# Elementwise bounds moved from VectorE to GpSimd, with new call lists, in a fused attention and feed-forward block on one core

## The chip, the cores and the metric

The kernel runs on one core of a Trainium2 chip. The metric is the device time in microseconds (us) of one execution. The engines are TensorE (PE; its weight loads are a row of their own, PEld), VectorE (DVE), ScalarE (ACT), GpSimd (POOL) and SyncE (SP), which here only issues DMAs. Each engine works through its own list of instructions in order; semaphores order the engines against each other.

## What is computed

The input `x` has 4 batches of 256 tokens with 256 channels. Two stages each add to it:

```python
def _bi_wkv(r, k, v, w, u, time_emb):            # k = v = fside, time_emb = cond
    tf = sigmoid(sum(time_emb, -1))[:, None, None]
    decay = exp(-exp(w))[None, :] * (0.5 + 0.5 * tf[:, :, 0])
    ek = exp(minimum(k, 30.0));  ekv = ek * v
    # forward and backward recurrences a = a*decay + ekv, b = b*decay + ek over the tokens
    euk = exp(minimum(u + k, 30.0))
    num = nf + nb - ekv + euk * v
    den = df + db - ek + euk
    return sigmoid(r) * (num / maximum(den, 1e-8)) * (0.8 + 0.2 * tf)

x = x + attn(_bi_wkv(x, fside, fside, w1, u1, cond), ...)   # Mamba-2 style: in_proj, causal conv, SiLU,
                                                           # 8 heads, decayed causal scores, RMS norm, gate, out_proj
x = x + ffn(_bi_wkv(x, fside, fside, w2, u2, cond), ...)    # ternary weights, 8-bit activations,
                                                           # 256 -> 1024, SiLU, GELU, layer norm, 1024 -> 256
# weight_quant: round(w / mean|w|) clipped to -1..1
```

The kernel applies `minimum(k, 30)` after the exponential, as a minimum with exp(30).

## The kernel before

The work is split by batch `b` = 0 to 3, and from the residual on by row block `i` = 0 to 7 of 128 tokens (two for each batch). Every engine has a set of small functions, one for each step, and under them a list of calls, which is the order of its work. The list of each engine mixes steps of different batches, so that the feed-forward of batch 0 runs beside the attention of batches 1 to 3. Nothing else orders the work: an engine whose next call waits for a semaphore does nothing until it comes. `HOME` gives each TensorE result its PSUM bank.

The steps that this document speaks of, in the order of the data:

- ACT `wkv_exp(b)` (L691) writes `E`, the exponential of `k`, one instruction of 128x512. ACT `wkv_own(b)` (L698) writes `own`, exp(u+k) for both stages, four instructions.
- DVE `wkv_min(b)` (L1192, its instruction L1195) and `own_min(b)` (L1197, L1199) bound the two with exp(30), one instruction each. POOL `times_v(b)` (L476, L480) and `own_times_v(b)` (L483, L487) multiply them with `v`. Only one pair of buffers exists for each, so a pair serves batches b and b+2.
- DVE `forward(b, w, k)` and `backward(b, w, k)` are the recurrences, each a scan of 128x514 (L1209, L1218), four of each for a batch: w is the stage, k the denominator (0) or the numerator (1). `forward(b, w, 0)` waits for the bound, `forward(b, w, 1)` for the product with `v`. They also wait for `D`, the decay factors, made for batches 1 to 3 by ACT `make_D` and `make_turn`, the latter from POOL `turn_decay` and DVE `make_decay` and `make_gap`. `add_own` (L1229) joins them with `own` into `nd`.
- ACT `recip_seed` (L734 to L738), DVE `recip` (L1237, L1240), `ratio` (L1246) and POOL `second_ratio` (L493) divide. ACT `gate_x` (L744) makes tanh(x/2), and DVE `gated(b)` (L1256) writes `uT`, the input of the attention part, on which TensorE's `features(b)`, `conv_in` and `gate_in` wait.
- From PE `features(b)` ACT and DVE make scores' factors and, through `softplus_log` and `softplus_out`, the log decays `la`. PE `running_sums(b)` sums them, ACT and DVE `running_sums(b)` split the sums, SP `spread_sums(b)` copies them into `cum_t` with six DMAs (L347), and PE `log_decays(b, c, g)` waits for them. PE `scores(b)` waits for the masks `late` and `tri` of POOL. ACT `decays` takes exponentials (L836), DVE `attend` (L1326) multiplies, PE `within` and `between` make the output, with POOL `state_values` (L500) before `between`.
- DVE `conv_taps` (L1302) is the convolution, six instructions for half a batch.
- `residual(p)`, `gate_h`, `ffn_in`, `norm_h` (POOL, L504 to L526), `ffn_in_scale`, `quantise_h` (POOL, L534) and PE `q1_turns(p)` prepare the feed-forward input of part p (batches 0 to 2 whole, batch 3 in two halves: p = 3 and 4). PE `ffn_up(i)` needs POOL `ffn_diag(i)` (L474); ACT `ffn_silu`, `ffn_gelu`, `ffn_var`, DVE `ffn_center`, `ffn_shift`, `ffn_max`, ACT `ffn_square`, POOL `ffn_dev`, `ffn_rms`, `ffn_round` (L568), SP `turn_q2(i)` (a DMA transpose), PE `ffn_down(i)`, DVE `ffn_out(i)` and SP `store(i)` are the rest.
- Both weights lie in `wn`. ACT `weight_abs(i)` (L683) sums their absolute values, PE `weight_sums`, DVE `weight_mean`, POOL `weight_round(i)` (L466), DVE `clip_weights(i)` (L1188, L1190) and ACT `weight_done(i)` (L689) quantise them, each instruction 128x2048.

PE `warm(k)` are eight matmuls on constants whose result nobody reads. ACT's functions come from several table sets; a `preload_act_table_set` call loads one (24 of them before).

The lists stand at L347 and after for SP, L571 for POOL, L927 for ACT, L1449 for DVE, L1834 for PE. Two pieces of the lists before, around the places that the prediction comes to:

```python
# ACT, first part                     # POOL, middle
recip_seed(0, 0, 1)                   state_values(2)
weight_abs(0)                         ffn_dev(0)
recip_seed(0, 1, 2)                   norm_h(1)
make_D(1)                             quantise_h(1)
```

## Time and profile before

| | |
|---|---|
| median of 3 runs | 205.1 us (204.43 to 205.75) |
| the profiled execution: its time | 205.91 us |
| its span, first to last instruction | 203.8 us |
| mean granted TensorE clock | 0.908 |
| instructions | 3179 |

The profile is of one execution, which took 0.8 us more than the median of the runs; 2.1 us of its time lie outside the span. Times in the rows are microseconds from the start of the span, unless marked ns.

### The profile page before, as it was taken

The page shows a single profiled execution, that of the slowest core. Times are in us where ns is not written, and L with a number is a line of the kernel's source. Part 1 is how long each engine was busy: PE and PEld are TensorE (multiplying, and loading weights), DVE is VectorE, ACT ScalarE, POOL GpSimd, SP SyncE. Part 2 cuts the span into 40 slices and gives each one's busy share as a digit, 9 for nine tenths or more (in the row PEclk, how much of TensorE's full clock was granted, in tenths as well). Part 3 has the DMA queues.
Part 4 walks back from the last instruction along what each step waited for, and adds up shares of the span by engine and source line. Part 5 has one row for each costly group of instructions (what it writes and reads, how often), then busy time and mean ns, then how long its engine had stood idle before and what let it go on. Part 6 is the DMA issues. An engine that isn't in the chain of part 4 may idle for free.

```text
span 203.8 us, 3179 instructions
## 1 busy us (share of the span) xinstructions
PE 163.1 (80%) x904; PEld 120.7 (59%) x908; DVE 178.1 (87%) x315; ACT 162.2 (80%) x295; POOL 100.5 (49%) x172
## 2 busy tenths in 40 slices
...
DVE  1899999999999999999999999998667777986952
...
GB/s 114 365 387 396 238 2 2 3 0 2 206 0 3 0 0 2 5 2 0 2 4 1 0 0 0 5 0 0 47 12 0 51 0 10 68 31 116 64 77 51
DMA packets 12304, 11.55 MB, mean 57 GB/s; under 512 B 7680, under 2 KB 10368, under 8 KB 12032
## 3 DMA queue, kind: packets, MB, share of 16 engines
...
q8 instruction: 7, 0.11, 0.2%
q10 hardware_dynamic: 432, 0.03, 0.2%
...
## 4 chain that ended last, share of the span: by engine, by line
PE 60%; DVE 19%; issue 8%; ACT 7%; POOL 4%; POOLq 1%; DVEq 0%; ACTq 0%
PE banks L1659 55%; PE banks L1656 5%; DVE Fs L1209 4%; DVE Ys L1218 4%; DVE nd L1229 2%; DVE banks L1409 1%; DVE decay L1153 1%; DVE wn L1417 1%; DVE tn L1237 1%; POOL wn L568 1%; ACT banks L890 1%; ACT banks L886 1%; ACT wn L912 1%; POOL gap_r L438 1%; DVE dtp L1282 1%
## 5 line engine op out<-in xcount | busy, mean ns | idle before, releaser
L1659 PE MATMUL banks<-inw,uT 128*128 128x8 f32 (+1 forms) x64 | 20.4, 444 | 16.7 <-DVE uT L1256 16.7
L1659 PEld LDWEIGHTS banks<-inw,uT 128*128 128x128 f32 x64 | 11.2, 215 | 23.0 <-issue 22.6
L1209 DVE TENSOR_TENSOR_SCAN Fs<-D,E 128x514 f32<-128x514 f32 x16 | 21.0, 1334 | 0.6 <-POOL D L441 0.5
L1659 PE MATMUL banks<-uT,inw 128*128 128x256 f32 x80 | 20.2, 397 | 0.0
L1302 DVE SCALAR_TENSOR_TENSOR cv<-banks,cols,cv 128x255 f32<-128x255 f32 (+2 forms) x48 | 19.3, 470 | 0.0
L1218 DVE TENSOR_TENSOR_SCAN Ys<-D,Fs 128x514 f32<-128x514 f32 x16 | 18.9, 1203 | 0.0
L500 POOL TENSOR_TENSOR vs<-vv,grow 128x512 f32<-128x512 f32 x4 | 4.5, 1131 | 28.5 <-issue 18.3
L1659 PEld LDWEIGHTS banks<-uT,inw 128*128 128x128 f32 x80 | 15.2, 197 | 3.1 <-issue 1.4
L1659 PEld LDWEIGHTS banks<-vv,skips 128*128 128x128 f32 x128 | 15.2, 192 | 2.1 <-issue 2.0
L1659 PE MATMUL banks<-w2T,wn 128*128 128x256 f16 x64 | 10.4, 320 | 7.6 <-DMA wn<-wn 7.6
L1659 PE MATMUL banks<-b1b,diag 128*128 128x512 f32 x32 | 15.1, 595 | 0.6 <-POOL diag L474 0.6
L1659 PE MATMUL banks<-vv,skips 128*128 128x64 f32 x128 | 15.4, 274 | 0.3 <-ACT vv L794 0.3
L1659 PE MATMUL banks<-vv,dec 128*128 128x64 f32 x128 | 15.6, 275 | 0.0
L1659 PEld LDWEIGHTS banks<-vv,dec 128*128 128x128 f32 x128 | 14.9, 192 | 0.0
L1659 PE MATMUL banks<-outw,yzT 128*128 128x256 f32 x64 | 14.7, 380 | 0.0
L1659 PE MATMUL banks<-starts 128*128 128x256 bf16 x80 | 12.7, 324 | 2.0 <-POOL starts L421 2.0
L1659 PEld LDWEIGHTS banks<-w2T,wn 128*128 128x128 f16 x64 | 7.3, 116 | 10.6 <-DMA wn<-wn 7.9
L1409 DVE SCALAR_TENSOR_TENSOR banks<-banks,nmu,xcT 128x1024 f32<-128x1024 f32 x8 | 10.3, 1288 | 3.2 <-issue 2.5
L1659 PEld LDWEIGHTS banks<-outw,yzT 128*128 128x128 f32 x64 | 11.8, 190 | 1.9 <-issue 0.5
L480 POOL TENSOR_TENSOR E<-E,vT 128x512 f32<-128x512 f32 x4 | 5.8, 1456 | 13.1 <-DVE E L1195 13.1
L487 POOL TENSOR_TENSOR own<-own,vT 128x1024 f32<-128x1024 f32 x4 | 11.2, 2790 | 1.7 <-DVE own L1199 1.7
L1659 PEld LDWEIGHTS banks<-starts 128*128 128x128 bf16 x80 | 9.1, 116 | 4.3 <-POOL starts L421 2.0
...
## 6 DMA issues: line engine op xcount, KB each, us to landing
...
```

Of the source, the lines that this page charges most:

```text
L438: pool.tensor_tensor(gap_r[:, :, :, 0], gap[:, :, :, 0], mhalf[:, 0:2 * CT].rearrange("p (w c) -> p w c", w=2), ALU.pow).then_inc(turn_ok, 1)
L480: pool.tensor_tensor(E[:, b % 2, 1, :, 0:T], E[:, b % 2, 0, :, 0:T], vT[:, b].rearrange("p (c t) -> p c t", c=CT), ALU.mult).then_inc(ev_o ...
L487: pool.tensor_tensor(own[:, b % 2, :, 1, :], own_e(b), vT[:, b].unsqueeze(1).broadcast_to([P, 2, CT * T]), ALU.mult)\
L500: pool.tensor_tensor(by_head(vs[:]), by_head(vv[:, b % 2, 0]), grow[:, 0, :].unsqueeze(2).broadcast_to([P, NH, HD]), ALU.mult).then_inc(vs ...
L568: pool.tensor_scalar(Q2[:, i % 2], Y[:, i % 2], qq[:, i:i + 1], ROUND16, ALU.mult, ALU.add)\
L1209: dve.tensor_tensor_scan(Fs[:, w, k], D[:, w, 0:CT * TS], E[:, b % 2, k].rearrange("p c t -> p (c t)"), 0.0, ALU.mult, ALU.add).then_inc(f ...
L1218: dve.tensor_tensor_scan(Ys[:, w, k][:, ::-1], D[:, w, 1:CT * TS + 1][:, ::-1], Fs[:, w, k][:, ::-1], 0.0, ALU.mult, ALU.add).then_inc(ys_ ...
L1229: last = dve.scalar_tensor_tensor(nd[:, :, w, s], y, gap[:, w, ct, b:b + 1], own[:, b % 2, w, :, s], ALU.mult, ALU.add)
L1302: dve.scalar_tensor_tensor(cv[:, ft, back:], at("conv_in", b, i)[:, j * T:(j + 1) * T - back], cols[:, w:w + 1], cv[:, ft, back:], ALU.mul ...
L1409: dve.scalar_tensor_tensor(ffn_mid(i), ffn_mid(i), nmu[:, i:i + 1], lngb, ALU.add, ALU.mult)\
L1656: return pe.transpose(dst, src, ident[0:n, 0:n])
L1659: return pe.matmul(dst, lhsT, rhs, start=start, stop=stop)
```

## The change

1. `wkv_min(b)` for b = 1 to 3 and `own_min(b)` for b = 1 to 3 run on POOL, as a tensor_scalar with two operations (minimum with exp(30), maximum with 0). `wkv_min(0)` and `own_min(0)` stay on DVE. The POOL functions wait in addition for the bound of the batch before.
2. `clip_weights(0)` and `clip_weights(1)` run on POOL.
3. The call lists of SP, POOL, ACT, DVE and PE are new throughout, and with them the PSUM banks in `HOME` and the bare waits between PE's calls. Nothing else of the functions changes. There are 25 table loads on ACT: two more in the first part, one less around `ffn_gelu(2)`.

The diff, cut to what the text speaks of:

```diff
 # SP: order of the loads
 load_cond()
 load_k(0)
-load_xT(0)
-load_x(1)
+load_b1()
+load_x(2)
 load_xT(2)
 load_k(1)
-load_x(2)
 load_k(2)
+load_w1()
+load_x(0)
+load_x(1)
 load_xT(1)
...
+load_xT(3)
+load_xT(0)
+load_w2()
+load_inw()
+spread_sums(0)
+load_k(3)
+load_b2()
...
 turn_q2(0)
 turn_q2(1)
+store(0)
 turn_q2(2)
 turn_q2(3)
+turn_q2(4)
 store(1)
-store(0)
+turn_q2(5)
 store(2)
-turn_q2(4)
-turn_q2(5)

 # POOL
+def clip_weights(i):
+    pool.wait_ge(wrnd_ok[i], 1)
+    pool.tensor_scalar(wn[:, i], wn[:, i], ROUND + 1.0, ROUND - 1.0, ALU.min, ALU.max).then_inc(wclip_ok[i], 1)
+
+def wkv_min(b):
+    pool.wait_ge(e_ok, b + 1)
+    pool.wait_ge(emin_ok, b)
+    e = E[:, b % 2, 0, :, 0:T]
+    pool.tensor_scalar(e, e, EXP_MAX, 0.0, ALU.min, ALU.max).then_inc(emin_ok, 1)
+
+def own_min(b):
+    pool.wait_ge(own_ok, b + 1)
+    pool.wait_ge(omin_ok, b)
+    pool.tensor_scalar(own_e(b), own_e(b), EXP_MAX, 0.0, ALU.min, ALU.max).then_inc(omin_ok, 1)
...
-make_ident()
 make_starts()
 make_masks()
+make_late()
+make_ident()
 first_turn()
 times_v(0)
 own_times_v(0)
-make_rows()
 turn_decay()
+wkv_min(1)
 times_v(1)
+own_min(1)
 make_tri()
+own_times_v(1)
 second_ratio(0)
-own_times_v(1)
+make_rows()
+wkv_min(2)
 times_v(2)
-make_late()
 second_ratio(1)
+own_min(2)
+wkv_min(3)
 state_values(0)
...
 norm_y(0, 0)
+weight_round(0)
 norm_y(0, 1)
-weight_round(0)
 state_values(1)
+own_min(3)
+residual_bias(0)
+clip_weights(0)
 times_v(3)
...
 state_values(2)
+weight_round(1)
 ffn_dev(0)
+clip_weights(1)
 norm_h(1)
+norm_y(2, 0)
 quantise_h(1)
...
 quantise_h(3)
-ffn_round(2)
 ffn_round(3)
+ffn_dev(4)
 ffn_diag(6)
-ffn_dev(4)
 norm_h(4)
 quantise_h(4)

 # ACT, first part
 wkv_exp(0)
+spread_heads()
+wkv_exp(1)
 wkv_own(0)
 wkv_own(1)
...
+weight_abs(0)
+act.preload_act_table_set("natural_log_exp_and_others")
+recip_seed(0, 0, 1)
+make_D(1)
+make_turn(1)
+recip_seed(0, 1, 2)
+act.preload_act_table_set("exp_and_others")
 gate_x(0)
+make_skips()
+weight_abs(1)
+features(0)
+wkv_own(2)
 exp_a()
 act.preload_act_table_set("natural_log_exp_and_others")
...
 # ACT, around ffn_gelu(2)
 act.preload_act_table_set("silu_and_others")
+silu_z(3, 0)
 ffn_silu(2)
 running_sums(3)
+weight_columns()
+silu_conv(3, 0)
+turned_y(2, 1)
 act.preload_act_table_set("gelu_and_others")
 ffn_gelu(2)
-act.preload_act_table_set("silu_and_others")
-silu_z(3, 0)

 # DVE: clip_weights gone, wkv_min and own_min called for batch 0 alone; first part
+wkv_min(0)
+out_factor()
 first_D()
-wkv_min(0)
 forward(0, 0, 0)
-own_min(0)
-backward(0, 0, 0)
-make_decay()
 forward(0, 0, 1)
 forward(0, 1, 0)
+backward(0, 0, 0)
+own_min(0)
 backward(0, 0, 1)
+make_decay()
 forward(0, 1, 1)
+make_gap()
 add_own(0, 0)
 backward(0, 1, 0)
 backward(0, 1, 1)
-make_gap()
 add_own(0, 1)
-out_factor()
 recip(0, 0, 1)
-own_min(1)
 ratio(0)
-wkv_min(1)
+forward(1, 0, 0)
 gated(0)
 recip(0, 1, 2)
-forward(1, 0, 0)
 forward(1, 0, 1)
...
-softplus_in(0)
 features(0)
+forward(1, 1, 0)
+backward(1, 0, 0)
+softplus_in(0)
+forward(1, 1, 1)
+backward(1, 0, 1)
 softplus_out(0)
...
 running_sums(0)
-wkv_min(2)
 conv_taps(0, 1)
 recip(1, 0, 2)
 conv_taps(0, 0)
 ratio(1)
-own_min(2)
 gated(1)

 # PE, last part (before: ffn_down(0) ahead of project(4), ffn_down(1) and (2) ahead of ffn_up(7))
 ffn_up(5)
+project(4)
 ffn_down(0)
-project(4)
 q1_turns(3)
+ffn_down(1)
 ffn_up(6)
-ffn_down(1)
-ffn_down(2)
 q1_turns(4)
 ffn_up(7)
+ffn_down(2)
```

## Rows read from the trace of the kernel before

**Rows 1.** The page: busy time of the engines; DVE's busy tenths and DMA rate in 40 slices.

```profile
PE 163.1 (80%) x904; PEld 120.7 (59%) x908; DVE 178.1 (87%) x315; ACT 162.2 (80%) x295; POOL 100.5 (49%) x172
...
DVE  1899999999999999999999999998667777986952
...
GB/s 114 365 387 396 238 2 2 3 0 2 206 0 3 0 0 2 5 2 0 2 4 1 0 0 0 5 0 0 47 12 0 51 0 10 68 31 116 64 77 51
```

**Rows 2.** Stretches: from:to, length, busy time of each engine (x instructions), clock, DMA share, GB/s.

```profile
80.00:100.00 20.00, 20.00 (x129) 16.47 (x128) 19.67 (x37) 17.07 (x37) 15.72 (x16) 1.00 0.01 2
...
137.00:150.00 13.00, 12.97 (x56) 7.82 (x55) 9.57 (x17) 11.80 (x19) 6.15 (x10) 1.00 0.11 21
```

**Rows 3.** The chain that ended last, in order of time: start, us, what.

```profile
45.86 0.41 DVE cum_s L1321
46.27 0.35 DVE E L1195
48.18 0.30 POOL late L432
48.53 3.03 PE banks L1659 x11
51.69 1.44 PE banks L1659 x3
```

**Rows 4.** Groups of DVE instructions by shape: busy, mean ns of one.

```profile
L1218 DVE TENSOR_TENSOR_SCAN Ys<-D,Fs 128x514 f32<-128x514 f32 x16 | 18.9, 1203 | 0.0
L1199 DVE TENSOR_SCALAR own<-own 128x1024 f32<-128x1024 f32 x4 | 2.7, 677 | 0.0
L1190 DVE TENSOR_SCALAR wn<-wn 128x2048 f32<-128x2048 f32 x2 | 2.4, 1211 | 0.0
L1195 DVE TENSOR_SCALAR E<-E 128x512 f32<-128x512 f32 x4 | 1.7, 419 | 0.0
```

**Rows 5.** Groups of POOL instructions by shape, the nearest to the moved ones.

```profile
L534 POOL TENSOR_SCALAR h<-h,hq 128x256 f32<-128x256 f32 x8 | 4.7, 588 | 3.3 <-DVE hq L1387 3.3
L466 POOL TENSOR_SCALAR wn<-wn,wrec 128x2048 f32<-128x2048 f32 x2 | 3.9, 1974 | 0.7 <-DVE wrec L1186 0.5
```

**Rows 6.** Timeline of POOL and DVE side by side around 10 us: start, us.

```profile
10.46 3.19 POOL L487 TENSOR_TENSOR own<-own,vT 128x1024 f32<-128x1024 f32 x1 [1.75 <-DVE own L1199]
11.44 2.63 DVE L1153 TENSOR_SCALAR decay<-fdec,eew 128x3 f32<-128x3 f32 x4
```

**Rows 7.** Timeline of the first part, around `gated(0)`

```profile
11.91 0.61 ACT L744 ACTIVATE th<-xcT 128x512 f32<-128x512 f32 x1
...
12.64 1.28 ACT L940 ACT_TABLE_LOAD   x1
...
25.29 0.63 ACT L738 ACTIVATE Ys<-Ys 128x512 f32<-128x512 f32 x1
...
26.86 0.68 DVE L1256 SCALAR_TENSOR_TENSOR uT<-th,nd 128x512 f32<-128x512 f32 x1
...
33.03 0.84 DVE L1265 SCALAR_TENSOR_TENSOR bcf<-banks,bcr 64x256 f32<-64x256 f32 x2
...
33.76 2.43 ACT L815 ACTIVATE skips<-ident,heads 128x128 f32<-128x128 f32 x8
...
36.10 1.90 ACT L683 ACTIVATE dec<-wn 128x2048 f32<-128x2048 f32 x1
```

**Rows 8.** POOL's timeline around 117 us.

```profile
117.11 1.04 POOL L500 TENSOR_TENSOR vs<-vv,grow 128x512 f32<-128x512 f32 x1 [14.82 <-issue]
...
121.45 0.19 POOL L504 TENSOR_SCALAR hmv<-hss 128x2 f32<-128x2 f32 x1 [0.81 <-ACT yzT L874]
```

**Rows 9.** Timeline around 171 us, DVE and POOL.

```profile
166.66 0.42 DVE L1362 SCALAR_TENSOR_TENSOR h<-h,R 128x256 f32<-128x256 f32 x1 [1.22 <-ACT h L862]
...
170.64 2.32 POOL L568 TENSOR_SCALAR wn<-wn,qq 128x1024 f16<-128x1024 f32 x2
...
171.95 1.28 DVE L1362 SCALAR_TENSOR_TENSOR h<-h,R 128x256 f32<-128x256 f32 x1
```

More of the change, by code:

```diff
@@ L30 @@
 HOME = {
-    "warm": (6, 2, 1, 5, 0, 4, 4, 3, 3, 6),
+    "warm": (7, 3, 2, 0, 6, 2, 4, 2, 5, 0),
     "cond_sum": 1,
-    "weight_sums": 7,
-    "features": (7, 2, 1, 3),
-    "conv_in": ((5, 2), (5, 6), (4, 2), (0, 4)),
-    "conv_turns": ((2, 5), (7, 5), (5, 2), (3, 2)),
-    "gate_in": ((0, 6), (6, 4), (7, 4), (2, 5)),
-    "r2_turns": (4, 0, 5, 4),
-    "scores": (1, 3, 3, 4),
-    "log_decays": (((7, 4), (3, 7)), ((1, 6), (7, 4)), ((5, 1), (0, 2)), ((2, 3), (6, 7))),
-    "running_sums": (3, 1, 1, 1),
-    "within": ((4, 2), (5, 6), (5, 2), (6, 5)),
-    "between": (3, 5, 4, 3),
-    "y_turns": ((3, 1), (2, 0), (7, 2), (2, 4)),
-    "project": (2, 2, 4, 3, 5),
-    "q1_turns": (3, 6, 7, 3, 6),
-    "ffn_up": (6, 0, 6, 0, 6, 0, 4, 6),
+    "weight_sums": 2,
+    "features": (0, 3, 6, 3),
+    "conv_in": ((5, 3), (6, 6), (2, 7), (4, 2)),
+    "conv_turns": ((6, 5), (1, 6), (4, 3), (3, 4)),
+    "gate_in": ((4, 0), (0, 3), (3, 2), (2, 5)),
+    "r2_turns": (7, 5, 5, 3),
+    "scores": (1, 5, 5, 2),
+    "log_decays": (((4, 6), (3, 4)), ((2, 4), (1, 0)), ((1, 0), (4, 3)), ((4, 3), (3, 6))),
+    "running_sums": (6, 1, 1, 4),
+    "within": ((7, 7), (2, 4), (4, 5), (7, 4)),
+    "between": (3, 7, 3, 2),
+    "y_turns": ((4, 4), (0, 4), (6, 0), (5, 5)),
+    "project": (7, 3, 1, 2, 4),
+    "q1_turns": (7, 7, 6, 2, 4),
+    "ffn_up": (6, 0, 6, 0, 6, 0, 2, 6),
     "weight_columns": 5,
-    "ffn_turns": ((0, 0), (0, 0), (0, 0), (0, 0), (0, 0), (0, 0), (3, 4), (5, 6)),
-    "ffn_down": (2, 2, 3, 0, 1, 2, 7, 0),
+    "ffn_turns": ((0, 0), (0, 0), (0, 0), (0, 0), (0, 0), (0, 0), (2, 3), (6, 7)),
+    "ffn_down": (3, 5, 4, 0, 1, 5, 4, 0),
 }
```

475 lines of the change are left out of this document (222 added, 253 removed).

## The prediction

> **What bounds the kernel now.** I read the page first, then stretches, then the chain, then timelines.
>
> The page [rows 1] shows no single bound: DVE is busy 87% of the span, PE and ACT 80%, POOL 49%. DVE's slices say when: nines from about 8 us to 138 us, sixes and sevens after that. The change takes work off DVE, so the question is whether DVE sets the end while it is full. The stretches [rows 2] answer it: from 80 to 100 us PE is busy 20.00 of 20 us at full clock, and DVE 19.67. Both are full. The chain [rows 3] runs through DVE up to 46 us (the split of the running sums, then a bound of `E`), through POOL's mask `late`, and from 48.53 us on PE, which it does not leave for long before 168 us. The list of PE's work is the same in sum before and after. So from 50 to 168 us a freed DVE gives nothing unless PE gets its work in another order or sooner, and the places to cost are the first 50 us, the steps that PE waits for, and the tail.
>
> **Part 1: the bounds and the clip leave DVE.** DVE loses three bounds of `own` (3 x 0.677), three of `E` (3 x 0.419) and two clips (2 x 1.211): 2.03 + 1.26 + 2.42 = 5.7 us [rows 4]. POOL gains the same eight instructions. No row shows a minimum on POOL. The nearest has the size and form of the clip: 1.974 us for 128x2048 [rows 5], by columns 0.99 us for 1024 and 0.49 us for 512, in sum 2 x 1.97 + 3 x 0.99 + 3 x 0.49 = 8.4 us. The other end is the 128x256 row, 0.588 us [rows 5], which by columns gives 4.70, 2.35 and 1.18, in sum 20 us. I take 8.4, since its row is of the clip's own size. POOL has 103 us free, so the sum fits; where it stands in the queue matters (below). On DVE, 1.1 of the 5.7 us stand before `gated(0)` (bounds of batch 1) and 4.6 later. What it is worth: at least 0, since PE covers it; at most 4.6 less the holds that the new POOL work puts on DVE.
>
> Such holds are in the trace: while POOL multiplied `own` from 10.46 to 13.65 us, four DVE instructions of three elements took 2.63 us together and ended 0.4 us after it [rows 6]; four more places look so. The Trainium skill, page "SBUF — State Buffer", section "Who interferes with whom", says that a DVE instruction with two SBUF inputs and a GpSimd instruction that reads SBUF exclude each other for the whole instruction. By that rule each moved bound that falls among scans holds DVE longer (0.99 us) than it did on DVE (0.677); by the rows of the three-element instructions alone one would expect a hold only now and then. It is a rival below.
>
> **Part 2: the first part, by the new lists.** Up to `add_own(0, 1)` DVE has the same work, in another order. The second seed on ACT, three steps of 0.63, follows it and ended at 25.92 [rows 7], so `add_own(0, 1)` ended at 24.0, and does now. From there to `uT` at 26.86 [rows 7] stood `recip(0, 0, 1)`, `ratio(0)` and two bounds (1.1), so the first two are 1.8 us. With `forward(1, 0, 0)` (1.2, as the other scans of [rows 4]) they end at 27.0. `gated(0)` also waits for tanh, and ACT's second seed has no reason to end sooner than 25.9. Behind it come a table load (1.28) and `gate_x(0)` (0.61) [rows 7], which before was done at 12.5: 25.9 + 1.3 + 0.6 = 27.8. `uT` of batch 0 starts at 27.8 to 28.2 instead of 26.86, 1.0 to 1.3 us late. ACT then makes the skips (2.43, [rows 7]) and the second weight sum (about 2.1) before `features(0)`, which starts near 32.7 and lets DVE's `features(0)` start at about 33.6 instead of 33.03 [rows 7]. DVE idles some 2 us before it. From there to the end of `add_own(1, 1)` stand four forward and backward pairs less the two forwards done (six scans, 7.2 us), and the short softplus and `add_own(1)`, which I estimate from the sizes in [rows 4] at 0.8 and 2.7: 33.6 + 0.8 + 7.2 + 0.8 + 2.7 = 45.1. Before, it ended at about 45.1 too, since the split of the sums behind it (1.2 us) ended at 46.27 [rows 3]. The relief of 1.1 us is spent on the wait for tanh. The loads: `in_w` comes last but one now, yet all loads together were through by 25 us (five slices of 5.1 us, [rows 1]), before PE needs it at 28.
>
> PE waited for `late` until 48.53 [rows 3], since POOL stood in its queue behind a bound of DVE. Now `late` is made at once. But the next step, `log_decays(0)`, waits for the sums that DVE ended at 46.27 and for six DMAs, and started at 51.69 [rows 3]. DVE ends those sums at 46.2 again, so the DMAs and `log_decays(0)` come at 51.6. Scores done early only lengthen the wait. Part 2 is worth 0; bounds: 1.1 us sooner (if tanh is not late) and 2 us later (if DVE's idle time adds to the wait).
>
> **Part 3: the middle.** The new lists load one table less around `ffn_gelu(2)`: 1.28 us of ACT (row of [rows 7]), in a stretch where ACT is busy 11.80 of 13 us but PE 12.97 of 13 [rows 2]. Between 0 and 1.28 I take the middle, 0.6 us gained. The two loads more in the first part are in part 2.
>
> **Part 4: the tail.** `ffn_in(4)` on DVE took 1.28 us beside POOL's two roundings, 170.64 to 172.96 [rows 9]; the other instruction of its size took 0.42 [rows 9]. Now one of the two is done sooner, so of the 0.86 us held I take 0.6 as gained, between 0 and 0.86. `project(4)` ahead of `ffn_down(0)` ends 1 us sooner on PE, but ACT reaches `gate_h(4)` only after `ffn_gelu(4)`, which waits for `ffn_up(5)` whose place is the same: 0. `store(1)` now stands behind the transposes of blocks 2 to 4 and the waits of their roundings; `ffn_out(3)`, which needs its buffer, is called after them: 0.
>
> **Sum.** 0 + 0 - 0.6 - 0.6 = -1.2 us. On the profiled execution 205.91 - 1.2 = 204.7, a span of 202.6; that execution was 0.8 above the median, so the median comes to 205.1 - 1.2 = 203.9 us. A change below 1% (2.05 us) is about what a measurement of this kernel can't tell from none, and this is below it. With the bounds of the parts the likeliest case itself reaches from 202 (1.1 + 1.28 + 0.86 = 3.2 gained) to 207.1 (2 lost).
>
> **Rivals.**
> - Rival A, the relief shows. If PE's fullness is one that follows DVE (PE gets each batch as DVE delivers it), 4.6 us come off, less two bounds of `own` that hold scans for 0.99 each: 2.6 net, and the 1.2 above: 201.3 us. For it: DVE is full from 8 to 138 us, the chain before 46 us is DVE's, and the lists are new on all engines, so PE may get the next batch sooner. Against: PE shows no idle time at all in [rows 2]. In its best form (all 4.6 and 1.2) 199.3.
> - Rival B, POOL's queue becomes late: the slower side. At 117.11 us POOL starts `state_values(2)`, having waited; `norm_h(1)` follows at 121.45 with 0.81 us to spare [rows 8]. Now `weight_round(1)` and `clip_weights(1)`, 1.97 each, stand between them, so `norm_h(1)` starts 3.9 - 0.8 = 3.1 us later, then `quantise_h(1)`, `q1_turns(1)` and the blocks 2 and 3 of the feed-forward, which PE's list has in a fixed place; `weight_done(1)` on ACT also waits. If PE stands still for it: 205.1 + 3.1 - 0.6 = 207.6 us (part 4's gain is kept). It decides when `state_values(2)` starts later than about 114 us. For it: POOL idled 14.8 us before 117.11 and now puts the work behind that wait instead of into it. Against: PE has `conv_in(3)` and `features(3)` to do meanwhile.
> - Rival C, the exclusion: of the 8.4 us of new POOL work, the part of batches 1 and 2 (2 x 0.99 + 2 x 0.49 = 3.0 us) falls where DVE does little but scans, and holds it in full, against 2 x (0.677 + 0.419) = 2.2 saved. DVE's first 60 us then get 0.8 us longer, and with the late tanh not covered (1.3) and -1.2: 205.1 + 0.8 + 1.3 - 1.2 = 206.0 us. For it [rows 6]; against, other POOL work beside scans left them at 1.2 us. This is what the rule of the skill named above would do here, and the trace agrees with it in part.
>
> **Chances.** Forecast 0.40, A 0.31, B 0.17, C 0.12. Faster by over 1% (below 203.05): 0.04 from the forecast's lower end, 0.28 from A, in sum 0.32. Slower by over 1% (above 207.15): 0.02, 0.15 from B, 0.05 from C, in sum 0.22. The rest, 0.46, is within 1%. The range that leaves 2 in 10 out reaches to A's centre and a little under it, and to B's: 200.5 to 207.7 us.
>
> **What the changed profile would show.** Part 1: DVE busy near 172 us; POOL near 109, with the clip at 1.9 to 2.1 us; the bounds at 1.0 and 0.5. If the clip is over 4 us, the cost of POOL is wrong and B grows. Part 2: `uT` first written at about 28 us with DVE idle before it, released by ACT's tanh; `add_own(1, 1)` ending near 45 us; the first `log_decays` near 51.6. Sooner than 50 refutes part 2 and speaks for A. Part 3: one table load less from 137 to 150 us, PE full from 57 to 167 us. PE idle for over 2 us before `ffn_up(2)` or `q1_turns(1)` would be B. Part 4: `ffn_in(4)` at 0.42 us. If PE stays without idle time and yet its last `ffn_up` ends over 3 us sooner than before, my reading of PE as the bound was wrong.

## The result, and the profile after

The changed kernel takes 209.8 us (median; runs 207.91, 209.81 and 209.89) against 205.1 us: a ratio of 1.0185 with an interval of 1.0129 to 1.0242. Measured again later, six runs lay between 208.0 and 210.2 us, beside eleven of the kernel before from 204.4 to 206.9: 1.0174 (1.0122 to 1.0226). The profiled execution took 209.89 us, its span is 207.8. It is nearly 2% slower; 203.9 was forecast, and 209.8 lies outside the range. Below, a time is the median of all runs of a kernel, and the brackets behind it give the ratio to the kernel before with its 95% interval. The ratio leaves out runs over 1.5% above the fastest of their kernel, so the two can stand apart, most of all in `g_tail` and `g_warm`, where 7 of 12 and 9 of 13 runs are left out.

The page of the kernel after, busy time of the engines as in [rows 1]:

```profile
span 207.8 us, 3188 instructions
PE 162.0 (78%) x903; PEld 119.1 (57%) x908; DVE 175.2 (84%) x307; ACT 164.1 (79%) x296; POOL 118.1 (57%) x180
```

DVE lost its eight instructions and POOL has eight more, 17.6 us of busy time instead of the 8.4 forecast; the span is 4.0 us longer. Groups of instructions by shape, after (busy, mean ns of one), beside [rows 4, 5]:

```profile
L478 POOL TENSOR_SCALAR wn<-wn 128x2048 f32<-128x2048 f32 x2 | 4.6, 2296 | 0.2
L489 POOL TENSOR_SCALAR own<-own 128x1024 f32<-128x1024 f32 x3 | 3.8, 1251 | 0.3
L484 POOL TENSOR_SCALAR E<-E 128x512 f32<-128x512 f32 x3 | 2.6, 854 | 18.3 <-ACT E L718 18.2
```

The moved work itself is 4.6 + 3.8 + 2.6 = 11.0 us, including the time in which it was held itself (a hold is time by which an instruction beside one of the other engine takes longer than it does alone). Most of the other 6.6 us comes from one instruction on 128x1 that otherwise takes 0.19 us and here took 8.44; some other rows of POOL are shorter than before. Timeline of POOL and DVE, after:

```profile
104.26 8.44 POOL L519 TENSOR_SCALAR ymv<-yss 128x1 f32<-128x1 f32 x1
104.34 1.20 DVE L1231 TENSOR_TENSOR_SCAN Fs<-D,E 128x514 f32<-128x514 f32 x1
...
109.95 2.70 DVE L1251 SCALAR_TENSOR_TENSOR nd<-Ys,gap,own 128x512 f32<-128x512 f32 x4
```

It began 0.08 us before a run of back-to-back scans and ended 0.05 us after the last product behind them.

Where does the time of the end come from? I read the same milestones in both timelines (ends, in us):

```
                         before  after  later by
uT of batch 0              27.5   31.3   3.7
add_own(1, 1)              45.1   47.6   2.5
split of the sums, b 0     46.3   49.3   3.0
within(1)                  95.9   99.2   3.3
within(2)                 126.2  129.8   3.6
within(3)                 159.6  163.5   3.8
project(3)                164.8  168.2   3.4
ffn_up(7)                 181.0  184.4   3.4
span                      203.8  207.8   4.0
```

The loss is there at 50 us and is only carried from then on: PE is busy 19.96 of 20 us from 80 to 100 us, as full as in [rows 2], and can catch up nothing. The last half microsecond is in the last two products, both `ffn_down`: they took 1.84 us each, at a granted clock of 1.2 GHz, and 1.72 and 1.04 us in the kernel before.

The trace of the later repetition (210.17 us, span 208.4) has DVE's work within 0.1 us of the first up to 60 us, and `log_decays` starts at 54.70 in both. But its clock comes back to 2.4 GHz at about 64.2 us and not at 58.1, so that `ffn_up(7)` ends at 186.6, 2.2 us later still, and then its last two products run at 2.4 GHz, 1.04 us each, which gives 1.6 us back. So 3.0 us of the loss are in the order of the work and stand in both traces; what comes on top of them changes with the clock from run to run.

The stretch that loses it, around `gated(0)`, POOL and DVE side by side, after; it answers to [rows 7]:

```profile
22.72 0.99 POOL L484 TENSOR_SCALAR E<-E 128x512 f32<-128x512 f32 x1
23.16 1.09 DVE L1259 SCALAR_TENSOR_TENSOR tn<-nd,Ys 128x512 f32<-128x512 f32 x1
23.79 1.58 POOL L495 TENSOR_TENSOR E<-E,vT 128x512 f32<-128x512 f32 x1
24.28 1.64 DVE L1262 SCALAR_TENSOR_TENSOR Ys<-tn,Ys 128x512 f32<-128x512 f32 x1
25.46 1.36 POOL L489 TENSOR_SCALAR own<-own 128x1024 f32<-128x1024 f32 x1
25.95 1.40 DVE L1268 SCALAR_TENSOR_TENSOR nd<-nd,fout,Ys 128x512 f32<-128x512 f32 x1
27.28 1.31 DVE L1231 TENSOR_TENSOR_SCAN Fs<-D,E 128x514 f32<-128x514 f32 x1
27.48 3.25 POOL L502 TENSOR_TENSOR own<-own,vT 128x1024 f32<-128x1024 f32 x1
28.51 2.76 DVE L1278 SCALAR_TENSOR_TENSOR uT<-th,nd 128x512 f32<-128x512 f32 x1
```

Read it as a handing over of turns. Each DVE instruction with two inputs ends 0.53 to 0.55 us after the POOL instruction beside it: `tn` at 24.25 after 23.71, `Ys` at 25.92 after 25.37, the ratio at 27.35 after 26.82, and `uT` at 31.27 after 30.73. Alone they take 0.69, 0.69, 0.74 and 0.68 us, as the same four do in the kernel before, where nothing of POOL of that kind stands beside them. These four and the scan took 8.2 instead of 4.0 us.

From `tn` on, the kernel before has such holds as well, 3.0 us of them, but all behind `uT`: `tn` of 1.75 us, two scans of 3.19 instead of 2.3 us, and a product of 128x16, `dtp`, of 1.31 instead of 0.15 us. Timeline of DVE, before:

```profile
27.46 1.75 DVE L1237 SCALAR_TENSOR_TENSOR tn<-nd,Ys 128x512 f32<-128x512 f32 x1
...
29.85 3.19 DVE L1209 TENSOR_TENSOR_SCAN Fs<-D,E 128x514 f32<-128x514 f32 x2
```

That difference in place is the one that counts. PE waits for `uT` to make the features of batch 0, and DVE needs those features about 5 us later. The chain that ended last, after (start, us, what), in the place of [rows 3]:

```profile
28.51 2.77 DVE uT L1278
...
31.42 3.77 PE banks L1671 x12
...
44.49 3.06 DVE nd L1251 x4
...
52.89 1.68 DMA cum_t<-cum_s
...
54.70 2.30 PE banks L1671 x5
```

And the two ends of it in the timeline, DVE idle for the features, PE for the decays:

```profile
36.08 0.85 DVE L1287 SCALAR_TENSOR_TENSOR bcf<-banks,bcr 64x256 f32<-64x256 f32 x2 [2.33 <-ACT bcr L782]
...
47.92 0.91 DVE L1341 CAST cum_s<-crest 40x256 bf16<-40x256 f32 x1
...
54.70 0.58 PE L1671 MATMUL banks<-cum_t,cum_s 99*128 99x512 bf16 x1 [7.73 <-DMA cum_t<-cum_s]
```

The sum, from the start of `tn` to the end of the split: DVE began `tn` at 23.16, 0.76 us sooner than before. Holds were 4.6 us (the 4.2 above and 0.35 in `add_own`) instead of 3.0 (+1.6), two bounds are gone (-1.1), DVE idled 2.33 us for the features (+2.3), and the cast of the sums took 0.91 instead of 0.28 us beside POOL's bound and product of batch 2 (+0.6). That is 1.6 - 1.1 + 2.3 + 0.6 - 0.8 = 2.6 of the 3.0 us. The 2.3 us of idle time are not a result of the held `uT`: they are 2.33 us as well in `e_product_later` below, where `uT` isn't held. They come with the new list, which gives DVE 2.6 us of work between `uT` and the features and not the 5.5 us (holds included) of the kernel before.

### The profile page after: what moved, and what is told of

Read it like the earlier page. It is cut to its first block, busy times and chain, and to the rows that moved or that the text cites. A ratio compares the mean times of both kernels' runs of the same rounds, so it can differ in the third digit from the quotient of the medians.

```text
span 207.8 us, 3188 instructions
## 1 busy us (share of the span) xinstructions
PE 162.0 (78%) x903; PEld 119.1 (57%) x908; DVE 175.2 (84%) x307; ACT 164.1 (79%) x296; POOL 118.1 (57%) x180
## 4 chain that ended last, share of the span: by engine, by line
PE 44%; DVE 21%; issue 10%; ACT 8%; POOL 8%; SPq 3%; DMA 3%; POOLq 1%; DVEq 0%; ACTq 0%
PE banks L1671 40%; DVE Fs L1231 4%; PE banks L1668 3%; DVE Ys L1240 3%; SPq L347 3%; DVE nd L1251 2%; DVE dec L1348 2%; POOL wn L583 2%; DMA cum_t<-cum_s 2%; DMA wn<-wn 1%; DVE uT L1278 1%; DVE decay L1178 1%; DVE cv L1324 1%; ACT vv L817 1%; POOL grs L521 1%
## 5 line engine op out<-in xcount | busy, mean ns | idle before, releaser
L1671 PE MATMUL banks<-inw,uT 128*128 128x8 f32 (+1 forms) x64 | 19.8, 435 | 19.9 <-DVE uT L1278 19.9
L1671 PEld LDWEIGHTS banks<-inw,uT 128*128 128x128 f32 x64 | 10.5, 208 | 24.7 <-issue 24.5
L1671 PE MATMUL banks<-uT,inw 128*128 128x256 f32 x80 | 21.6, 415 | 0.0
L1671 PEld LDWEIGHTS banks<-uT,inw 128*128 128x128 f32 x80 | 16.1, 209 | 3.9 <-issue 1.9
L1671 PE MATMUL banks<-w2T,wn 128*128 128x256 f16 x64 | 11.2, 335 | 5.3 <-DMA wn<-wn 5.3
L1671 PE MATMUL banks<-cum_t,cum_s 99*128 99x512 bf16 x16 | 7.0, 439 | 8.5 <-DMA cum_t<-cum_s 8.4
L484 POOL TENSOR_SCALAR E<-E 128x512 f32<-128x512 f32 x3 | 2.6, 854 | 18.3 <-ACT E L718 18.2
L1671 PE MATMUL banks<-starts 128*128 128x256 bf16 x80 | 11.7, 315 | 1.3 <-POOL starts L421 1.3
L583 POOL TENSOR_SCALAR wn<-wn,qq 128x1024 f16<-128x1024 f32 x8 | 9.1, 1134 | 4.6 <-DVE qq L1453 4.3
```

What stands on the lines that cost most here:

```text
L484: pool.tensor_scalar(e, e, EXP_MAX, 0.0, ALU.min, ALU.max).then_inc(emin_ok, 1)
L583: pool.tensor_scalar(Q2[:, i % 2], Y[:, i % 2], qq[:, i:i + 1], ROUND16, ALU.mult, ALU.add)\
L1671: return pe.matmul(dst, lhsT, rhs, start=start, stop=stop)
```

## The experiments

All change the call lists or the engine of a bound; what is computed stays the same except where said. "Bounds of batch b" are `wkv_min(b)` and `own_min(b)`.

**The two halves of the change apart.** The move without the new lists, and the new lists without the move:

```diff
# e_move_alone, on the kernel before
 VectorE's list:  -wkv_min(1), (2), (3)  -own_min(1), (2), (3)  -clip_weights(0), (1)
 GpSimd's list:   +each of them directly ahead of the call that reads it
# e_lists_alone, on the changed kernel
 GpSimd's list:   -the same eight calls
 VectorE's list:  +the same eight, behind the calls that they followed in the old list
```

> The old call lists, only the bounds of batches 1 to 3 and both clips moved to GpSimd, each right in front of the step on GpSimd that needs it. Theory M (the loss comes from GpSimd work that holds DVE's two-input instructions in front of uT of batch 0, where the new lists bunch it): here own_times_v(1) stands behind second_ratio(0), so uT of batch 0 is written at 27.5 to 28.5 us and the time is 204 to 207 us. Theory L (the lists are harmless, the moved work itself costs the 4 us): 208 us or more. Theory Q (GpSimd's queue around 117 us is late): no q1_turns(1) delay here, 204 to 206 us.

> The new call lists, with all bounds and clips back on DVE near their old places (5.7 us of DVE work back, 8.4 us off GpSimd). Theory M: own_times_v(1) still stands in front of uT of batch 0, so about 2 us of its delay stay, and about 1.3 us of holds go against 1.1 us of DVE work: 208 to 211 us. Theory L (the moved work costs): 205 us.

Measured: the move alone 211.2 us (1.024, 1.018 to 1.030), the lists alone 213.2 us (1.033, 1.028 to 1.039). Both halves lose, each more than both together (1.0185), so no half of the change carries the loss, and on the new lists the move brings 3.4 us. Theory M, with 204 to 207 and 208 to 211 us, missed both; theory L fits the first and not the second. Where each loses, from the timelines. The move alone, 79 to 93 us, where the clip and the bound of batch 3 stand beside `gated(2)`:

```profile
79.86 3.03 POOL L478 TENSOR_SCALAR wn<-wn 128x2048 f32<-128x2048 f32 x1
...
79.92 1.22 DVE L1260 SCALAR_TENSOR_TENSOR tn<-nd,Ys 128x1024 f32<-128x1024 f32 x1
81.17 2.80 DVE L1263 SCALAR_TENSOR_TENSOR Ys<-tn,Ys 128x1024 f32<-128x1024 f32 x1
...
86.12 1.65 DVE L1279 SCALAR_TENSOR_TENSOR uT<-th,nd 128x512 f32<-128x512 f32 x1
...
87.93 3.46 PE L1674 MATMUL banks<-uT,inw 128*128 128x256 f32 x8 [1.86 <-DVE uT L1279]
```

Here both sides are held in turn: POOL's clip (1.90 us in its undisturbed place) waits for `tn`, and `Ys` (1.23 us before) waits for the clip. `uT` of batch 2 ends at 87.8 instead of 83.7, PE stands still for 1.86 us, and the eight products behind the gap take 3.46 instead of 1.89 us, at 1.2 GHz. The lists alone, POOL's work of batch 0 and the product of batch 2 beside DVE's scans:

```profile
58.40 3.27 POOL L502 TENSOR_TENSOR own<-own,vT 128x1024 f32<-128x1024 f32 x1
59.45 3.31 DVE L1226 TENSOR_TENSOR_SCAN Fs<-D,E 128x514 f32<-128x514 f32 x1
...
66.25 3.67 PE L1674 MATMUL banks<-vv,dec 128*128 128x64 f32 x16 [3.59 <-DVE dec L1343]
```

The same mechanism at a third place: a scan of 1.2 us takes 3.31, and PE waits 3.59 us behind it. The first part of this kernel is as fast as that of the kernel before (`log_decays` starts at 51.5, before 51.7) and 3.2 us ahead of the changed kernel; this wait and the 1.2 GHz behind it (3.67 us for products that take 2.00 in the changed kernel) lose all of it. A good start alone saves nothing here.

**The product, and the bounds, in front of `uT` of batch 0.** Two parts of the change undone alone, and then both:

```diff
# e_product_later, on the changed kernel, GpSimd's list
 make_tri()
-own_times_v(1)
 second_ratio(0)
+own_times_v(1)
# e_bounds1_dve, on the changed kernel
 GpSimd's list:   -wkv_min(1)  -own_min(1)
 VectorE's list, behind recip(0, 0, 1):
+own_min(1)
 ratio(0)
+wkv_min(1)
# f_both: the two together
```

> The changed kernel with own_times_v(1) behind second_ratio(0) on GpSimd, as in the old list. Theory M: the 2.76 us of uT's instruction of batch 0 fall to 0.7, PE starts its features at 29.3 us instead of 31.4, and the 2 us show at the end if DVE's chain behind it moves up too: 206.5 to 208.5 us. Theory T (late tanh on ACT is what holds uT, whose table load and tanh end at 27.55): no change, 209.8 us.

> The changed kernel with the two bounds of batch 1 back on DVE between recip and forward of batch 1, the rest as changed. Theory M with equal exchange: GpSimd loses 2.3 us in front of uT of batch 0, DVE gains 1.1: uT of batch 0 0.5 to 1.5 us sooner, 208.3 to 209.5 us. Theory Q or T: no change or 1 us more, 209.8 to 211 us.

> The changed kernel with both mends: bounds of batch 1 on DVE and own_times_v(1) behind second_ratio(0). Theory M (each GpSimd step that reads SBUF beside two-input DVE instructions in front of uT of batch 0 holds them): the two mends overlap, since either takes one hold of over 1 us away from uT; together uT of batch 0 ends at 28.3 to 29.0 us and the time is 204.5 to 206.5 us. If they were independent causes their gains would add (3.3 + 3.9 us) and give 202.6 us.

Measured: the product later 206.5 us (1.004, 1.000 to 1.008); the bounds of batch 1 back on DVE 205.9 us (1.001, 0.998 to 1.004). Each alone takes back 3.3 to 3.9 of the 4.7 us; for the bounds I had expected 208.3 to 209.5. In the traces the first part accounts for 2.1 and 2.4 us of it, the distance to the changed kernel at `within(1)`. The span with the bounds back is shorter by 4.0 us because its last two products ran at 2.4 GHz, 1.04 us each instead of 1.84, which is the clock and not the change. `uT` and its neighbour, first with the product later, then with the bounds back:

```profile
28.50 0.66 DVE L1278 SCALAR_TENSOR_TENSOR uT<-th,nd 128x512 f32<-128x512 f32 x1
```

```profile
26.23 2.24 POOL L495 TENSOR_TENSOR E<-E,vT 128x512 f32<-128x512 f32 x1 [3.61 <-DVE E L1218]
27.57 1.45 DVE L1279 SCALAR_TENSOR_TENSOR uT<-th,nd 128x512 f32<-128x512 f32 x1 [0.16 <-ACT th L765]
```

With the product out of its way `uT` starts at the same 28.50 and takes 0.66 us instead of 2.76, so 2.1 us of the 3.7 are that one product. With the bounds on DVE, POOL's products come when DVE lets them, and `uT` ends at 29.0; the product of `own`, still ahead of `second_ratio(0)`, starts at 29.14, behind `uT`. The first product of PE that needs `cum_t` begins at 52.6 and 52.5 us instead of 54.7. The gains don't add: both together gave 207.9 us (1.008, 1.004 to 1.013), outside both of my expectations, of ten runs four from 205.4 to 206.0 and six from 207.9 to 208.2; `log_decays` starts at 52.5 as with the bounds alone. The profiled run of it has the upper time, and shows what sets the two apart. PE after the decays of batch 0, with the bounds alone back, and below it with both:

```profile
57.10 1.29 PE L1674 MATMUL banks<-inw,uT 128*128 128x8 f32 x8
58.24 1.11 PE L1674 MATMUL banks<-uT,inw 128*128 128x256 f32 x4
59.19 1.88 PE L1674 MATMUL banks<-inw,uT 128*128 128x512 f32 x4
```

```profile
57.12 1.72 PE L1674 MATMUL banks<-inw,uT 128*128 128x8 f32 x8
58.69 2.05 PE L1674 MATMUL banks<-uT,inw 128*128 128x256 f32 x4
60.53 2.64 PE L1674 MATMUL banks<-inw,uT 128*128 128x512 f32 x4
```

The same work starts at the same time. In both the granted clock had fallen to 1.2 GHz in PE's wait for `cum_t`; in the one it is back at 2.4 GHz at about 57.8 us, in the other at 62.0, within the 2.64 row; the block behind them starts at 63.00 instead of 60.90, and `ffn_up(7)` ends 2.0 us later. What makes the clock come back at one moment or the other isn't shown. In the changed kernel's own trace it came back by 58.8 us (0.96 for the first of these rows), so its 3.0 us are not of this kind.

**The product without the bounds.** The changed kernel, with the bounds of batch 1 on POOL cut to one column each (the rest of batch 1 is left unbounded):

```diff
+if b == 1: e = e[:, :, 0:1]              # in wkv_min
+if b == 1: o = own_e(b)[:, :, 0:1]       # in own_min
```

> The changed kernel, the two GpSimd bounds of batch 1 cut to one column each (the rest of batch 1 is left unbounded), the product of own still ahead of second_ratio(0). Theory M with a race for who comes first: own_times_v(1) then starts about 1.5 us sooner (25.9 instead of 27.5), still in front of uT; DVE's ratio and scan of batch 1 are held instead. uT of batch 0 ends 1 to 2 us sooner than 31.27, the time is 208.0 to 209 us. If the bounds alone were the cause it would be 205.9 as with the bounds on DVE, or less.

Measured 208.0 us (1.013, 1.007 to 1.020), and in the trace:

```profile
27.00 3.24 POOL L507 TENSOR_TENSOR own<-own,vT 128x1024 f32<-128x1024 f32 x1
28.17 2.62 DVE L1283 SCALAR_TENSOR_TENSOR uT<-th,nd 128x512 f32<-128x512 f32 x1
```

`uT` still ends at 30.8, held by the product, which started at 27.0 and not at 25.9 as expected. DVE began `tn` 0.6 us later in this trace than in the changed kernel's, so the bounds' own time on POOL is worth about 1.1 us at `uT`, and the product in front of it the larger part. Together with `e_product_later` and `e_bounds1_dve` this says: `uT` is held by about 2 us when the product of `own` starts just in front of it, as the new list has it, and not when it starts behind.

**Tanh early, and the bound of batch 2.** My forecast blamed tanh behind a table load. `f_tanh` is `f_both` with it out of the way, and `f_tanh_bound2` with the bound of batch 2 away from the cast of the sums:

```diff
# f_tanh, on f_both
 ScalarE's list:
 weight_abs(0)
+gate_x(0)
 preload natural_log_exp_and_others
 ...
 recip_seed(0, 1, 2)
-preload exp_and_others
-gate_x(0)
 make_skips()
 ...
 exp_a()
-preload natural_log_exp_and_others
 VectorE's list:
+gated(0)
 forward(1, 0, 0)
-gated(0)
# f_tanh_bound2, on f_tanh
 GpSimd's list:   -wkv_min(2)
 VectorE's list:  +wkv_min(2) behind running_sums(0)
```

> f_both with the first tanh in front of the seeds on ACT (two table loads less in the first part) and gated(0) in front of forward(1, 0, 0). The recorded prediction blamed the late tanh for 1.0 to 1.3 us. If it costs that, uT of batch 0 ends at 27 us or sooner and the time falls 1 us below f_both, 203.5 to 205.5 us; if DVE's features(0), which waits for ACT and PE, only waits longer, it is the same within 0.5 us.

> f_tanh with the bound of E of batch 2 on DVE too, behind the split of the sums. Theory M: GpSimd's bound and product of E for batch 2 start at 44 us beside add_own(1, 1) and the cast of the sums, which took 0.91 us instead of 0.29; without them there the split of the sums ends 0.6 to 1 us sooner, against 0.42 us of DVE work behind it: 0.5 us faster than f_tanh, 203 to 205 us.

Measured 207.3 us (1.008, 1.003 to 1.012) and 205.1 us (0.999, 0.995 to 1.003). The first missed its 203.5 to 205.5. `uT` ended at 28.3 and at 27.4 us. `f_tanh` is no clean test of the tanh: the new lists load `xT(0)` late, ACT stood 5.22 us for it in front of the early `gate_x(0)`, the seeds behind it came late, and DVE waited 1.45 us for them before `tn`:

```profile
20.77 0.63 ACT L765 ACTIVATE th<-xcT 128x512 f32<-128x512 f32 x1 [5.22 <-DMA xcT<-in_xT_dram]
...
24.70 0.69 DVE L1258 SCALAR_TENSOR_TENSOR tn<-nd,Ys 128x512 f32<-128x512 f32 x1 [1.45 <-ACT Ys L759]
```

In `f_tanh_bound2` the same load landed 0.9 us sooner, which is half of the 1.8 us by which its split ends before that of `f_tanh`; the other half fits the cast (0.6 us shorter) and `add_own` (0.35). In it the cast was back at 0.28 us, the split ended at 46.5, and `project(3)` at 164.9, each within 0.3 us of the kernel before, and so was the time. With the first part mended, the rest of the new lists together with the three bounds and two clips left on POOL show neither a gain nor a loss.

**The tail.** From `project(4)` to `ffn_up(7)` the changed kernel takes 11.5 us, the kernel before 10.4, and I took that 1 us for a loss of the tail.

```diff
# g_tail, on f_tanh_bound2
 ScalarE's list:
+square_h(4)
 ffn_gelu(5)
-square_h(4)
 GpSimd's list:
-ffn_dev(4)
 ffn_diag(6)
+ffn_dev(4)
 norm_h(4)
# h_tail_after (on the changed kernel) and h_tail_mend (on f_tanh_bound2)
 ScalarE's list as in g_tail; GpSimd's list:
-ffn_dev(4)
 ffn_diag(6)
 norm_h(4)
+ffn_dev(4)
 VectorE's list:
-ffn_shift(4)
 ffn_in_scale(4)
 ffn_in_back(4)
+ffn_shift(4)
# h_after_again: the changed kernel, unaltered
```

> The kernel of f_tanh_bound2 with the kernel of before's order at two places of the tail: on ScalarE square_h(4) ahead of ffn_gelu(5), on GpSimd ffn_diag(6) ahead of ffn_dev(4). Theory (the tail's own share of the loss is these two places): in f_tanh_bound2 project(4) ended 1.0 us earlier than in before and ffn_up(7) at the same 181.1, so 1.0 us was given back between them; with the old order q1_turns(4) and ffn_up(7) come about 1.0 us earlier (ffn_up(7) ends near 180.0), the end about 1 us earlier: 204.1, against 205.1 of f_tanh_bound2. Rival (rounds (4) and (5) on GpSimd and the last products set the end, and the gelu that is now later delays them): ffn_up(7) comes earlier and the end does not, 205 or later.

> The changed kernel once more, unaltered, on the chip and beside the runs of before that the next two share. Theory (a loss of 3.0 us in the first 50 us and about 1 us in the tail): all runs 207.5 to 210, ratio 1.015 to 1.022, and runs below 206.5 do not occur. Rival (the loss is a matter of two groups of times and the first three runs fell in the upper one): several of ten runs at 205.5 to 206.5, ratio below 1.01.

> The changed kernel with a corrected tail: ScalarE square_h(4) ahead of ffn_gelu(5); GpSimd ffn_diag(6), norm_h(4), then ffn_dev(4), so that nothing that waits for ffn_var(4) stands before the norm of the last tile's h (in g_tail it still did, hmv at 174.94 behind std 174.59); VectorE ffn_in_scale(4) and ffn_in_back(4) ahead of ffn_shift(4). Theory (the tail's own share of the loss is the order around h(4)): in the trace q1_turns(4) 180.7 comes at 178.5 to 179.5 and ffn_up(7) ends at 182 to 183 instead of 184.4; the end is 0.5 to 1.5 us earlier than that of the changed kernel, since rounds (4) and (5) of the hidden values start a little later. Rival (the end is set by the chain of ffn_mean to ffn_down of tiles 6 and 7 on ScalarE and VectorE, in which the maxima and rounds of (4) and (5) stand ahead): ffn_up(7) earlier and the time within 0.3 us of the changed kernel's.

> f_tanh_bound2 (first part as fast as in before) with the same corrected tail. Theory: the last milestone before the tail, project(4), ends near 169.6 as in f_tanh_bound2 (1.0 us before that of the kernel before), and now the tail keeps it: q1_turns(4) near 176, ffn_up(7) near 179.8, median 203.5 to 204.5, a ratio of 0.990 to 0.997. Rival (as above): 205, ratio 0.999, with ffn_up(7) earlier all the same.

Measured: `g_tail` 208.0 us (0.998, 0.993 to 1.003), its lowest run 204.6 against 204.3 of the kernel it was made from: no gain. The ratio rests on the five of twelve runs from 204.6 to 207.2; the other seven lie between 207.7 and 210.3, and why they are so many isn't shown. The repetition of the changed kernel gave the 1.0174 told above: a shift of all runs, four of them from 208.0 to 209.7 and two at 210.2. The corrected tails were slower: 210.9 us (1.026, 1.021 to 1.031) on the changed kernel, 210.7 us (1.026, 1.022 to 1.031) on the mended one. The trace of `h_tail_mend` shows PE and ACT in the tail:

```profile
180.09 1.15 ACT L932 ACTIVATE wn<-wn,grs 128x1024 f16<-128x1024 f32 x1 [1.69 <-DVE wn L1437]
...
181.24 0.36 ACT L900 ACTIVATE q1T<-banks 128x256 bf16<-128x256 f32 x1
...
181.70 1.30 PE L1672 MATMUL banks<-w1T,q1T 128*128 128x512 bf16 x4 [2.02 <-issue]
182.79 3.34 PE L1672 MATMUL banks<-b1b,diag 128*128 128x512 f32 x4
```

PE stands still for 2.02 us in front of `ffn_up(7)`, with no releaser shown, where 0.52 us was usual. The rows of ACT settle what it waits for: `ffn_up(7)` starts 0.1 us after ACT's `turned_q1(4)` (L900), its input. That stands in ACT's list behind `ffn_square(4)` (L932), which waited 1.69 us for DVE's `ffn_shift(4)`, put later by my own edit; in `f_tanh_bound2` the same step of ACT ended at 178.24 and `ffn_up(7)` started at 178.34. Behind the gap its last four products take 3.34 instead of 1.88 us, most of them at 1.2 GHz. In `h_tail_after` the same gap of 2.02 us cost no clock (1.88 us), and `ffn_up(7)` ended 1.0 us later than in the changed kernel. Of the 5.0 us by which `ffn_up(7)` is later in `h_tail_mend` than in `f_tanh_bound2`, 2.4 are there at `uT` of batch 2: the clock came back at about 62.8 us instead of 55.4. My theory of the tail falls. The 1 us isn't a loss: the new list of PE calls `project(4)` ahead of `ffn_down(0)`, which moves that milestone 1 us forward and nothing else. From `project(3)` to `ffn_up(7)` both kernels take 16.2 us.

**The clock in the wait.** Small matmuls that write only the bank which `log_decays(0, 0, 0)` overwrites, in PE's wait:

```diff
# g_warm, on g_tail, TensorE's list
 pe.wait_ge(zs_ok, 1)
+56 matmuls of 256 columns (starts by starts)
 log_decays(0, 0, 0)
# g_before_warm, on the kernel before, TensorE's list
 gate_in(0, 1)
+56 matmuls of 256 columns (starts by starts)
 scores(0)
```

> g_tail, and in TensorE's wait for the decays of batch 0 (45.2 to 51.9 us) 56 small matmuls into the bank that log_decays(0, 0, 0) will write, so that the engine is busy up to about 51 us. They add nothing to the output. Theory (the two groups of times 2 us apart come from the moment at which TensorE's granted clock goes back from 1.2 to 2.4 GHz after this wait): the clock stays at 2.4 GHz, the six products for log_decays(0) take about 0.38 instead of 0.63 us, features(1) starts sooner, and all ten runs lie in one group, 203 to 203.5 us, with none about 2 us above it. Rival (the groups have another cause, or the clock falls in spite of the matmuls): still some runs 2 us above the others, median as that of g_tail. Second rival (the 56 matmuls themselves run at 1.2 GHz, last 12 us and delay log_decays): 207 or more.

> The kernel of before with 56 such matmuls in its own wait (42.1 to 48.5 us), ahead of scores(0). Nothing of the output changes. Theory of the clock: the products from 48.5 to 56.3 us run at 2.4 GHz, the block of batch 1's features and gates begins about 0.5 to 1.5 us earlier (it waits for cum_t at 51.7 still), the later runs of before (up to 207.3) have no counterpart, and the median is 203.5 to 204.5. Rival (that stretch is hidden behind VectorE, which is busy throughout it): 205.1, no change, with the same spread.

Measured: 210.2 us (1.009, 1.003 to 1.014; over four of thirteen runs) on the mended kernel, 206.1 us (1.001, 0.998 to 1.004) on the kernel before. In `g_warm` the time is that of the second rival, but the filler didn't run at 1.2 GHz for 12 us. PE, in its wait:

```profile
40.06 1.10 PE L1672 MATMUL banks<-tri,la 128*72 128x128 f32 x4 [2.62 <-DVE la L1310]
...
49.65 5.69 PE L1672 MATMUL banks<-starts 128*128 128x256 bf16 x48
55.18 0.38 PE L1672 MATMUL banks<-never,identb 128*128 128x512 bf16 x1
```

PE had stood still for 2.62 us before 40.06 and was at 1.2 GHz from 40 to 50 us. The filler began at 47.94, ran its first 2.3 us at that clock and the rest at 2.4 GHz, took 7.4 us in all and delayed the decays by over 3 us. At full clock it takes 6.28 us (`g_before_warm`), and the wait that it was to fill is 4.1 us in `g_tail`: it was too long at either clock. The clock was indeed at 2.4 GHz afterwards, and still the runs spread from 206.7 to 211.9 us, against the theory of one group. In the kernel before, the filler kept the clock (granted 1.00 from 45 to 50 us instead of 0.62), `cum_t` came at the same time, and nothing was gained: the stretch waits for DVE's sums. The clock fell right behind it all the same (0.67 from 50 to 55 us), after a wait of 1.35 us. The theory that the clock's rise there sets the difference between runs was not confirmed for that kernel.

**Relief against holds, alone.** Last, two moves into the full first part and no others, and in another kernel two moves undone:

```diff
# i_front_only, on the kernel before
 VectorE's list:  -own_min(1)  -wkv_min(1)
 GpSimd's list:   +wkv_min(1) ahead of times_v(1)  +own_min(1) ahead of own_times_v(1)
# g_move_keep, on e_move_alone
 GpSimd's list:   -wkv_min(3)  -clip_weights(0)
 VectorE's list:  +both, at their places in the kernel before
```

> The kernel of before, old lists, with only wkv_min(1) and own_min(1) moved to GpSimd (ahead of times_v(1) and of own_times_v(1)); the other four bounds and the clips stay on VectorE. VectorE is rid of 1.1 us (0.42 and 0.68) in the first part, where it is busy without a gap. Theory of the holds: the 1.1 us come back as longer tn (1.10 instead of 0.69), Ys (1.64) and the first scan of batch 1 (3.28 for two instead of 2.3), as in e_move_alone; the last add_own of batch 1 ends at 45.5 to 46 (45.1 in before) and the time is 205.2 to 206.2, no gain. Rival (a VectorE instruction taken off a stretch where VectorE is full is a gain): the last add_own ends near 44.0, the log decays of batch 0 come 1 us earlier, 204.2.

> e_move_alone (old call lists) with two of its moved pieces back on VectorE at their old places: wkv_min(3) and clip_weights(0), those that stood beside Ys (81.17, 2.80 instead of 1.23), ratio(2) and uT(2) in its trace. The bounds 1, 2, own_min(3) and clip_weights(1) stay on GpSimd. Theory (the loss of the bare move is mostly the hold at 80 to 88 us): uT(2) ends at 83.5 to 84.5 as in before instead of 87.8, TensorE's gap of 1.86 us and its half clock behind it go, and the time is 205 to 207, against 211.2. Rival (the loss is spread over all moved pieces): 209 to 211.

Measured: `i_front_only` 206.0 us (1.004, 1.000 to 1.007). DVE behind `uT`:

```profile
26.81 1.10 DVE L1254 SCALAR_TENSOR_TENSOR tn<-nd,Ys 128x512 f32<-128x512 f32 x1
27.95 1.64 DVE L1257 SCALAR_TENSOR_TENSOR Ys<-tn,Ys 128x512 f32<-128x512 f32 x1
29.51 3.28 DVE L1226 TENSOR_TENSOR_SCAN Fs<-D,E 128x514 f32<-128x514 f32 x2
...
33.93 2.36 DVE L1307 SCALAR_TENSOR_TENSOR la<-dtp,expa 128x72 f32<-128x72 f32 x2
```

`uT` comes 0.6 us sooner, 26.9, and `add_own(1, 1)` 0.6 us later, 45.7: 1.1 us taken off a full DVE came back as 1.7 us of holds (even `la`, 0.38 before, took 2.36 beside POOL's product). `g_move_keep` gave 210.6 us (1.019, 1.012 to 1.026), near its rival: `uT` of batch 2 ended at 86.2, still 2.5 us late, 1.1 of it there already at `uT` of batch 1. The loss of the bare move is spread over the moved pieces.

## Why the prediction was wrong

**The bound: right.** PE is full from 57 to 167 us (busy 108.2 of 110) and freed DVE time there gave nothing that the traces show. That same reading, turned round, carries a loss: 3.0 us at 50 us were 3.4 at 165.

**Part 1: the moves right, the holds left at "at least 0".** DVE's busy time did not fall by 5.7 us but by 2.9. The clip took 1.90 us undisturbed (1.97 forecast), the bounds 1.04 and 0.61 at their shortest (0.99 and 0.49). The lower bound of 0 was false, since it rested on PE covering the moved work wherever it stood, and the first 30 us have no such cover: in the trace of `i_front_only` the relief there comes out at -0.6 us, with a ratio of 1.004 (1.000 to 1.007).

**Part 2: the step that failed.** It said that `uT` would start at 27.8 to 28.2 for want of tanh, and that the relief of 1.1 us would be spent on that wait. Tanh was there at 27.55, as forecast, and DVE came to `uT` only at 28.51, having been held four times, and was then held for 2.1 us more by `own_times_v(1)`, which the new list puts ahead of `second_ratio(0)`. I priced that instruction at nothing beside DVE though [rows 6] shows the same product holding DVE. In its place the runs showed: `uT` ends at 31.3 instead of 28.9 at the latest, 0.6 us are lost at the cast, and `log_decays` starts at 54.7 instead of 51.6. The 45.1 for `add_own(1, 1)` was 47.6. The bound of "2 us later" was short by 1. The rest of the path was right: with the product out of the way (`e_product_later`) DVE starts on the features at 33.96 (33.6 forecast), idles 2.33 us before them ("some 2 us") and ends `add_own(1, 1)` at 45.5 (45.1).

**Part 3.** ACT was busy 11.66 us from 137 to 150 us, 0.14 less than in [rows 2], and PE 12.89 of 13 (11.64 and 12.94 from 140.5 to 153.5, where the same work lies now): no 0.6 us.

**Part 4.** `ffn_in(4)` took 0.43 us, as forecast, in the place of the 1.28 of [rows 9]. It wasn't worth 0.6: the milestones behind it kept their distance.

**Rivals.** A fell: a later DVE made PE later, but a freed DVE did not make it sooner. B did not come: `norm_h(1)` started at 128.89, but released by ACT's `yzT`, not by POOL's queue; `q1_turns(1)` ended at 134.2 instead of 131.0, and the milestones around it are late by the same 3.2 to 3.6 us that came from the first part. C was the mechanism, at 0.12 and 206.0 us. Its condition, POOL work of batches 1 and 2 among scans and products, is what the traces show. Its size was wrong, since it counted only the 3.0 us of bounds as new work; the products `E*v` and `own*v` (1.27 and 2.35 us at their shortest, 1.6 and 3.3 here) hold DVE as well, and the lists moved one of them to in front of the instruction that PE waits for. What the prediction held against C, that POOL's work left the scans at 1.2 us, was a misreading: the kernel before has the two scans of 3.19 us shown above.

The Trainium skill, page "SBUF — State Buffer", section "Who interferes with whom", states that exclusion in both directions. The traces agree: `uT` 2.76 instead of 0.68 us on DVE's side, `ymv` 8.44 instead of 0.19 us on POOL's. I had weighed the rule by the three-element rows alone and called it half confirmed.

What stays open: the parts of the sum come to 2.6 of the 3.0 us; the 0.6 to 0.8 us by which `within(2)` and `within(3)` are later still weren't traced; and in some kernels (`f_both`, `f_tanh`, `i_front_only`, and most widely `g_tail` and `g_warm`) runs lie 2 us and more above the others. Two pairs of traces (`e_bounds1_dve` and `f_both`, the changed kernel and its repetition) tie 2 us to when the clock comes back; it was not brought under control. How much of the median loss of 4.7 us beyond the 3.0 is of this kind was not measured.
